# Attention kernel: sums of the diagonal tiles from a second column of ones, inverses one reduction later, blank rows cleared by VectorE

## The reference

```python
scores = jnp.einsum('bnhd,bmhd->bhnm', q, k) / jnp.sqrt(jnp.float32(Dh))
scores = jnp.where(causal, scores, neg)
scores_t = jnp.where(terrace_allowed, scores, neg)     # own segment and the one before
att_t = jax.nn.softmax(scores_t, axis=-1)
out_t = jnp.einsum('bhnm,bmhd->bhnd', att_t, v)
att = jax.nn.softmax(scores, axis=-1)                  # the whole causal row
awc = att.reshape(b, H, r, seg, L) * jnp.exp(index_decays)[None, :, None, :, None]
pcs = awc.sum(axis=-2)                                 # one row of sums per segment
...                                                    # decayed over segments, gives w
kv = jnp.einsum('bhrs,bshd,bshe->brhde', w, k, v)
y = tw * out_t + (1.0 - tw) * out_lin
```

## Time and profile before

| | |
|---|---|
| Median of 3 runs | 2676.49 us (2672.58 to 2676.88) |
| Profiled execution | 2675.66 us, its span 2674.0 us |
| Busy over the span | PE 2301.8 us (86%), DVE 1920.6 (72%), ACT 1564.0 (58%), POOL 1237.5 (46%) |
| Projection stage | about 0 to 127 us, DMA at 217 and 244 GB/s in its first two slices of 67 us |
| Attention stage | about 138 to 1249 us |
| Minima of the pieces, L668 DVE | 704 instructions, 611.5 us busy, 880 ns each |
| Exponentials of the pieces, L597 ACT | 704 instructions, 596.0 us busy, 848 ns each |
| Sums over queries, L813 PE, two kinds | 4864 and 1024 matmuls, 432.7 and 208.5 us busy |
| GpSimd's small operation L520 | 128 instructions of 212 ns |

### The profile page before, as it was taken

The page is one execution under the profiler, slowest core; times in us unless marked ns, Lnnn a source line. Parts: engine busy times, 40 slices in busy tenths (PEclk is TensorE's granted clock), DMA queues, the critical chain, the costliest instruction groups (busy, mean ns, idle before and its releaser), DMA issues. The chain is left out here.

```text
span 2674.0 us, 72919 instructions
## 1 busy us (share of the span) xinstructions
PE 2301.8 (86%) x27120; PEld 1535.0 (57%) x27120; DVE 1920.6 (72%) x4760; ACT 1564.0 (58%) x3827; POOL 1237.5 (46%) x2277
## 2 busy tenths in 40 slices
PE   8689999999999999997987944499999999688791
PEld 5435454454544544444756834377777777565681
DVE  6578888888888888884664656277777776476465
ACT  5467777777777777774352322366666665465230
POOL 3324444444444444445674536545544444247461
PEclk9879999999999999998898965699999999689896
DMA  6711111111112111112436644301111111553555
GB/s 217 244 47 38 39 38 39 39 36 38 35 37 65 36 37 38 39 38 83 147 121 205 219 163 170 108 21 50 50 46 50 50 40 32 173 190 122 144 156 200
DMA packets 187403, 243.45 MB, mean 91 GB/s; under 512 B 41400, under 2 KB 144709, under 8 KB 185136
## 3 DMA queue, kind: packets, MB, share of 16 engines
q1 hardware_dynamic: 160656, 182.07, 22.1%
q0 software_dynamic: 19872, 50.41, 5.5%
q10 hardware_dynamic: 6528, 6.31, 0.8%
HBM read 136.09 MB, written 106.50 MB: 91 GB/s over the span
## 5 line engine op out<-in xcount | busy, mean ns | idle before, releaser
L668 DVE TENSOR_REDUCE at_mn<-at_S 128x1 f32<-128x1024 f32 (+4 forms) x704 | 611.5, 880 | 113.5 <-PE at_S L773 107.9
L597 ACT ACTIVATE at_E<-at_S,at_mn 128x1024 f32<-128x1024 f32 (+4 forms) x704 | 596.0, 848 | 153.4 <-DVE at_mn L668 153.4
L813 PE MATMUL at_pcs<-at_E,at_c 128*32 128x256 f32 (+1 forms) x4864 | 432.7, 345 | 0.0
L773 PE MATMUL at_S<-at_sk,at_sq 96*128 96x512 bf16 (+3 forms) x1152 | 334.0, 354 | 37.0 <-ACT at_E L597 25.4
L546 POOL TENSOR_TENSOR at_kvo<-at_kh,at_vh 128x256 f32<-128x256 f32 x512 | 303.6, 627 | 0.0
L813 PEld LDWEIGHTS at_pcs<-at_E,at_c 128*32 128x32 f32 x4864 | 185.8, 108 | 86.5 <-issue 80.6
L587 ACT ACTIVATE at_Tt<-at_S,at_mn 128x192 f32<-128x192 f32 x512 | 173.2, 421 | 104.0 <-DVE at_mn L658 104.0
L1293 POOL DMA_INDIRECT expert_out<-m_ysb,m_dst x158 | 155.4, 984 | 131.5 <-DVE m_dst L1471 118.4
L813 PE MATMUL at_pcs<-at_Tt,at_c 128*32 128x128 f32 x1024 | 208.5, 286 | 0.0
L520 POOL TENSOR_TENSOR at_fr<-at_f,at_rs 128x12 f32<-128x12 f32 x128 | 27.2, 212 | 381.3 <-ACT at_f L602 381.3
L773 PEld LDWEIGHTS at_S<-at_sk,at_sq 96*128 96x128 bf16 x1152 | 78.6, 97 | 214.5 <-issue 91.9
(11 more groups left out here) (392 smaller groups left out, 5534.3 us busy)
## 6 DMA issues: line engine op xcount, KB each, us to landing
m_xg<-expert_rows SPq DMA_DIRECT2D x158, 129.0 KB
at_sq<-q_parts SPq DMA_DIRECT2D x192, 64.0 KB, 2.2
at_sk<-k_parts SPq DMA_DIRECT2D x192, 64.0 KB, 2.2
memory_rows<-m_blank SPq DMA_DIRECT2D x8, 1032.0 KB
gl_hx<-memory_rows SPq DMA_DIRECT2D x32, 258.0 KB, 3.8
m_wgu<-in_f_wgu SPq DMA_DIRECT2D x2, 4096.0 KB, 13.9
m_yin<-expert_out SPq DMA_DIRECT2D x8, 1024.0 KB, 6.9
rt_yin<-expert_out SPq DMA_DIRECT2D x7, 1024.0 KB, 10.2
```

What stands on the lines that cost most here:

```text
L597: nc.scalar.activation(E[:, at:at + w], S[v % NS_B][:, 0:w], ACT.Exp, bias=mn[:, q, s, 1 + j:2 + j], scale=-1.0, accum_out=rs[:, q, s, 1 + ...
L668: nc.vector.tensor_reduce(mn[:, q, s, 1 + j:2 + j], S[v % NS_B][:, 0:w], AX.X, ALU.min).then_inc(s_mn, 1)
L773: ins = nc.tensor.matmul(S[v % NS_B][:, c:c + cw], sq[:, u, t * P:(t + 1) * P], sk[:, u, c0 + c:c0 + c + cw], start=True, stop=True)
L813: ins = nc.tensor.matmul(pcs[j * R:(j + 1) * R, cols[0]:cols[1]].rearrange("p (b c) -> p b c", c=P), lhsT, rhs, start=(n, j) not in touche ...
```

## The change

1. **A second column of ones.** EV goes from 17 to 18. The new column is 1 in the first 64 rows of each value tile and 0 in the other 64. For the second half of a tile's queries the first column of ones already gives the sum over the diagonal tile; for the first half, whose window also holds the segment before, the new column does. `diag_sums` (L672) is gone; in its place `outputs` has two copies of 64 partitions by 4 elements from the PSUM buffer `M` into `rs`, ahead of the inverse `inv_t`. GpSimd's `weights` waits for both.
2. **Order on VectorE.** `inverses` moves from after the third piece, ahead of `outputs`, to after the fourth.
3. **Order on GpSimd.** The share of `kvo` products stands ahead of `weights`, not behind it.
4. **The last group.** `keep_transposed` and `outputs` come ahead of `inverses`.
5. **Blank rows.** The three memsets of `blank` go from GpSimd, ahead of its first indirect DMAs, to VectorE, behind `add_shared(NS - 1)` and ahead of the expert tiles.

```diff
-EV = DH + 1
+EV = DH + 2
...
+            v4 = vv[:, :, :, :].rearrange("p b h (t e) -> p (b h) t e", e=EV)
+            pool.memset(v4[:, :, :, DH:EV], 1.0).then_inc(ones_set, 1)
+            pool.wait_ge(ones_set, 1)
+            pool.memset(v4[SEG:P, :, :, DH + 1:EV], 0.0).then_inc(ones_set, 1)
+            pool.wait_ge(ones_set, 2)
...
-                    act.wait_ge(ones_set, 1)
+                    act.wait_ge(ones_set, 2)
...
-                pool.wait_ge(s_ds, g + 1)
+                pool.wait_ge(s_ds, 2 * g + 2)
...
-                weights(g)
                 if q == 3:
                     products(n, 0, 5)
...
+                weights(g)
...
-            def diag_sums(g):
-                dve.wait_ge(s_E, unit(g, 0) + 1)
-                nc.vector.tensor_reduce(rs[:, g % NQ, :, 0], Tt[:, g % NQ, :, SEG:TW], AX.X, ALU.add).then_inc(s_ds, 1)
...
                 dve.wait_ge(s_O, g + 1)
+                nc.vector.tensor_copy(rs[0:SEG, q, :, 0], o[0:SEG, :, DH + 1]).then_inc(s_ds, 1)
+                nc.vector.tensor_copy(rs[SEG:P, q, :, 0], o[SEG:P, :, DH]).then_inc(s_ds, 1)
                 nc.vector.reciprocal(inv_t[:, g % 2, :], o[:, :, DH]).then_inc(s_invt, 1)
...
                     if k == 3:
+                        outputs(g)
+                    if k == 4:
                         inverses(g)
-                        outputs(g)
...
                 if g + 1 == NG:
-                    inverses(g)
                     keep_transposed(g)
                     outputs(g)
+                    inverses(g)
...
-            if x_out is None:
-                pool.memset(blank[:, :, 0:D], 0.0).then_inc(blanked, 1)
...
             add_shared(NS - 1)
+            if x_out is None:
+                nc.vector.memset(blank[:, :, 0:D], 0.0).then_inc(blanked, 1)
...
```

More of the change, by code:

```diff
@@ L155, in _ @@
                                pattern=[[-1, P]], channel_multiplier=1).then_inc(made, 1)
-            pool.memset(vv[:, :, :, :].rearrange("p b h (t e) -> p (b h) t e", e=EV)[:, :, :, DH:EV], 1.0
-                        ).then_inc(ones_set, 1)
+            v4 = vv[:, :, :, :].rearrange("p b h (t e) -> p (b h) t e", e=EV)
[3 more added lines that the diff above has]
+            pool.wait_ge(ones_set, 2)
             for n in range(NS):
@@ L716, in _ @@
             tops(0)
-            diag_sums(0)
             for g in range(NG):
@@ L737, in _ @@
                     normalise(n - 1)
-                diag_sums(g + 1)
             normalise(NHEAD - 1)
@@ L1274, in _ @@
                 scale_of(k)
-            if x_out is None:
-                pool.memset(blank[:, :, 0:D], 0.0).then_inc(blanked, 1)
-                pool.memset(blank[:, :, D:D + 1], FAR).then_inc(blanked, 1)
-                pool.memset(blank[:, :, D + 1:XW], 0.0).then_inc(blanked, 2)
             for n in range(NS):
@@ L1466, in _ @@
             add_shared(NS - 1)
+            if x_out is None:
+                nc.vector.memset(blank[:, :, 0:D], 0.0).then_inc(blanked, 1)
+                nc.vector.memset(blank[:, :, D:D + 1], FAR).then_inc(blanked, 1)
+                nc.vector.memset(blank[:, :, D + 1:XW], 0.0).then_inc(blanked, 2)
             for t in range(NTILE + 2):
```

## The result

The changed kernel took 2699.93 us in the median of 4 runs (2697.20 to 2701.56), the kernel before 2676.68 (4 runs, 2672.58 to 2676.96): a ratio of 1.0089, 95% interval 1.0072 to 1.0107. It is slower by 23 us, where +5 was forecast. The profiled execution took 2701.56 us, its span 2699.8.

What follows compares the result with a forecast made beforehand. TensorE's list of work, with gaps, was taken to set the pace. Per head 0.30 + 0.26 - 0.18 - 0.21 = +0.17 us, times 32 is 5.4; with 0.3 and -0.4, +5.3: 2681.8 us, range 2662 to 2699.

Steps and rivals of the forecast that it cites:

- the two gaps that the prediction had counted: TensorE's gaps for transposed tiles in quarter 0 (0.18 us) and window exponentials in quarter 1 (0.21) close, per head.
- third rival: VectorE's relief is worth more: 2642 us if VectorE sets the pace, 2664 if only two gaps close; chance 0.20.
- ten times as long: Argument against VectorE setting the pace: it waits for TensorE 38.5 us, TensorE for its copy 2.1.
- The two copies: VectorE's two new PSUM copies on different partitions take 0.15 us each, with 0.16 from each to the next operation.
- The round trip: Copies, GpSimd's total, inverse: fifth piece at t + 1.25 us, t being when the third piece's reduction frees VectorE.
- A tie, 0: Quarter 1: the fifth piece starts at t + 1.25 us before and after, so no cost.
- quarter 2's +0.30: Quarter 2: the fifth piece waits behind the inverse and starts 0.30 us late, adding 0.30 per head.
- the sign that was named for it: Profile sign in quarter 2: the inverse, with the fifth piece behind it, waits about 0.2 us for GpSimd's total.
- Quarter 0: With the inverse at the end, the weights (`c2`) come late and TensorE waits 0.26 us more per head.
- Quarter 3 at nothing: Quarter 3: the late fifth piece costs 0, hidden by TensorE's whole `kvo` product; uncovered, at most 10 us in all.
- The end -0.4: End of the attention stage: reordered products and sooner last copies change the time by -0.4 us, bounds -2.9 and +1.5.
- each 0.1 us that the round trip takes longer costs 0.1 us here too: Quarter 1: a longer round trip lengthens TensorE's largest gap, 0.77 us, by the same amount.
- The first rival: The round trip decides: copies of 0.25 us, each held until the previous ends, cost 0.73 per head, 2700 us; chance 0.18.

Runs made afterwards that it cites:

- c1: x1 with a second copy of the same partitions ahead of the first, into a tile nobody reads: 2757.82 us against 2760.49, ratio 0.9988.
- x1: Changed kernel with the second column all ones and unwanted values zeroed or not loaded, so one copy serves all 128 partitions: 2669.64 us against 2678.58, ratio 0.9964.
- x4: Changed kernel with the three memsets of `blank` back on GpSimd: 2701.52 us against 2675.89, ratio 1.0096.
- d5: Kernel before with sixteen small VectorE copies ahead of quarter 1's fifth piece: 2831.70 us against 2758.13, ratio 1.025.
- d2: Kernel before with six small VectorE copies ahead of quarter 2's fifth piece: 2683.79 us against 2675.89, ratio 1.0029.
- p2: Changed kernel with TensorE's transposes and next sums (quarter 1) or sums alone (quarter 2) ahead of the next scores: 2670.69 us against 2675.89, ratio 0.9974.
- x5: Changed kernel with the inverse behind the fifth piece in quarter 1 alone: 2770.36 us against 2758.13, ratio 1.0046.
- d4: Kernel before with twelve small VectorE copies ahead of quarter 1's fifth piece: 2777.77 us against 2760.49, ratio 1.0064.
- d3: Kernel before with eight small VectorE copies ahead of quarter 1's fifth piece: 2760.01 us against 2760.49, ratio 1.000.
- x3: Changed kernel with the inverse behind the fifth piece in quarter 2 alone: 2692.07 us against 2678.58, ratio 1.0054.
- x2: Kernel before with the changed order alone, the diagonal sums staying a reduction: 2675.20 us against 2678.58, ratio 0.9985.
- d1: Kernel before with six small VectorE copies ahead of quarter 1's fifth piece: 2675.29 us against 2678.58, ratio 0.9988.

## Why the prediction was wrong

**Bound, and where to look: right.** TensorE's list with its gaps sets the pace; the 0.38 us per head can be read from its gaps, and VectorE's 12 us less of work in 200 were worth no more than the two gaps that the prediction had counted (third rival: wrong). Its "ten times as long" was eighteen (38.5 / 2.1).

**The two copies: right in kind, short in size.** 0.16 was taken, 0.18 and 0.20 measured; most of the cost is that they are held, the lesser part that there are two (c1: 0.13 us a head of 0.61).

**The round trip: the step that failed first.** GpSimd was given 0.07 us after VectorE's result, by the row of another of its operations, and took 0.14. With the copies' spacing this made t + 1.38 of t + 1.25. "A tie, 0" in quarter 1 was +0.10, quarter 2's +0.30 was +0.40. In quarter 2 the sign that was named for it, the inverse waiting 0.2 us for the total, is missing: the fourth piece, put at t + 0.84 (its terms give 0.83), came at t + 0.92 and was in the way for as long. Nor did the 0.40 appear in the wait for L614's copy, which stayed 0.23, but in that for the exponential, from 0.13 to 0.53. A tie worked out from terms that are each read to 0.05 us is not a zero; it is the place where every error is paid. All errors had the same sign here.

**Quarter 0: right.** 0.26 for the wait for `c2`, 0.22 measured; -0.18 and -0.21 came back to the last digit. Quarter 3 at nothing held as well: TensorE has no new gap there, and from its `inv_t` to that of quarter 0 it is 9.78 us after 10.08 before.

**Extra column, blank rows, end.** The column was taken as 0, and that held: from the first to the last value product of a group it is 0.43 us with 17 columns and with 18, and x1, which has the same column, has TensorE busy 32.36 us a head, less than the kernel before. So the 0.04 us more of busy time in the changed kernel is not the column's; what it is stays open. Blank rows 0: nothing shows against it (x4). The end -0.4: -0.65.

**The clock: not in the prediction at all.** The sentence that failed is "each 0.1 us that the round trip takes longer costs 0.1 us here too". The 0.10 us cost 3.2 us by their length, and behind that gap the clock fell in six heads, 13.4 us. d5 shows that quarter 1's gap alone can do it, d2 that 0.46 us in quarter 2 don't; with the gap shortened or split (x1, p2, x5) the profiles have no fall behind it, and one elsewhere (p2, last head). Why 0.87 us brought six is not shown, since 1.03 us in d4 brought one. The profile before could have warned: its clock was at 1.00 with a gap of 0.77 us in each head, and no row in it told how much longer the gap could be. Such a missing row is an unknown cost, and belonged into the range.

The first rival had 2700 and so the right total, but not for its reason. It had 0.73 us a head, all regular; 0.38 were regular, and the rest came by a way that no rival had.

**What stays open.** Which heads are hit: with a gap of 1.03 us d4 has one fall in 32 heads, with 0.79 us d3 has one too, with 0.87 us the changed kernel has six, and a gap of 1.16 us in x3 (at 612.21) has none behind it. So the gap's length is not the only condition. How many falls the runs without a profile had can only be guessed from their mean granted clock. In d4 it is 0.913 in the two faster runs and 0.910 and 0.909 in the two slower ones, 8 to 14 us longer. One fall takes 0.5 x 6.83 / 2772 = 0.0012 from it, so by this estimate the slower runs had some two or three falls more.

## What to carry to other kernels

Where a chain ends in a tie with the wait that it is to hide behind, price the case in which it is late by a tenth of a microsecond, and look first at what hangs on it. Small operations on VectorE that work on other partitions than their neighbours should be turned into one on all partitions, even if the data must be laid out anew for it: here this made a loss of 23 us a gain of 9. On a TensorE that is nearly always busy, look for the longest single gap and the granted clock together, and break that gap up before anything that could lengthen it is added (p2 did this for the changed kernel, and kept one fall of six).

## What the runs showed of the hardware

- The granted clock fell to 0.50 for 6.83 us in a stretch in which TensorE was busy 95% of the time, after single gaps of 0.87 to 1.27 us (once 0.79), 1.8 to 2.3 us after their end; once, in p2, after three gaps of 0.39, 0.23 and 0.27 us in a row. Each fall that a head's length shows cost 2.1 to 2.9 us. With gaps of 0.77 us (0.78 once in c1): none, up to the end of the stage, in the profiles of the kernel before, x1, x2, c1, d1 and d2.
- Falls in the 32 heads, by the gap of quarter 1: 1 at 0.79 (d3), 6, 6 and 4 at 0.87 (the changed kernel, x4, x3), 1 at 1.03 (d4), 20 at 1.27 (d5). The number does not follow the length alone.
- GpSimd's first operation of the chain started 0.14 us after the end of VectorE's copy (in x1 and c1 too), and 0.08 us after the end of ScalarE's factors `f` in the kernel before; its operation on an inverse started 0.07 to 0.08 us after the inverse's end. Why the copy takes longer to be seen is not shown.
- A small VectorE operation that starts on other partitions than the one in front (64 after 0, or 0 after 64) started 0.03 us after that one's end; on the same partitions, 0.07 to 0.08 us after its start (after, x1, c1).
- Copies of one column on VectorE, one after another, took 0.45 us for six.
